# A macaron block on one core: feed-forward weights rounded in nine blocks of columns, attention masks built one level per batch, the second part's small loads first

## The chip, the core and the metric

The kernel runs on one core of a Trainium2 chip. Its time is the device time in microseconds (us) of one execution; the figure compared is the median of several executions. The core has five engines with a queue of their own: TensorE (PE), VectorE (DVE), ScalarE (ACT), GpSimd (POOL) and SyncE (SP, which here only issues DMAs). They meet through semaphores; each works through its own queue in order.

## The reference

For x of 8 batches x 512 tokens x 256 channels:

```python
x = x + 0.5 * ffn(layernorm(x))      # gate, up 256 -> 768, silu(gate) * up, down 768 -> 256
x = x + attn(layernorm(x))           # gated delta rule, 16 heads of 128
x = x + 0.5 * ffn(layernorm(x))      # the same weights again
def _quantized_matmul(x, w, scale):
    wq = w.astype(jnp.float8_e4m3fn).astype(x.dtype)
    return jnp.einsum('bsi,io->bso', x, wq) * scale
```

The attention projects to q, k, v (with a causal convolution over 4 tokens and silu), a decay alpha and a strength beta per head, runs the delta rule over the 512 tokens, normalises per head, gates and projects back. The feed-forward weights (gate, up and down, 768 KB each in float32) are rounded to 8-bit floating-point values and kept as float16.

## The kernel before, in words

`macaron` calls `ffn_phase` (first part), `attention_phase` and `ffn_phase` again (second feed-forward part; `first` is False). A barrier of all engines stands between the three. `stream` holds all of x in SBUF throughout.

**A feed-forward part** goes over 8 batches of 512 tokens. For a batch: DVE takes statistics (`stats`, L355 and L359), POOL makes 1/sqrt and shift (`root`, L271 to L276), ACT normalises (`normed`, L497), PE turns (`z_turned`, L606), ACT and DVE write it as two float16 halves (`high` L509, `low` L371). Then for each of six column blocks m of the 768: PE `gate` and `up` (L634, four 128x512 matmuls each), ACT `silu` (L517), DVE `hidden` (L380, the product with the up scale), ACT `hidden_high` (L526) and POOL `low` (L284) its two halves, PE `down` (L652). At the end DVE `added` (L391) scales and POOL `added` (L294) adds to `stream`. PE keeps three banks for gate and up; `hid`, `hh` and `hl` are rings of HB = 3. The order on each engine is written out by hand in `turn1(b)` (first part) and `turn2(b)` (second). In the first part a turn also prepares the attention for the batch before (index 1 of `root`, `normed` and so on, and the decays), and takes up to three weight jobs: SP loads a head's 128 KB into one of four slots (`load_job`, L1564), ACT splits off the high half (`high_job`, L1587 and L1589), POOL the low half (`low_job`, L1597).

**The start of the first part.** DVE rounds the three weights, one after the other, six chained instructions on 128x1536 each (L457 to L464; `s_wd` counts them), with batch 0's `low` and batch 1's statistics after the first; then the small weights of the decays (L470 to L472) and the halved down scale (L477), then `hidden(0, 0)`. SP issues the loads in the order of L156 to L187: weights, tokens, small ones, the convolution's parameters; then it waits for all the rounding (L182), saves the rounded weights to DRAM for the second feed-forward part (L183), and only then loads the first weight jobs. ACT's order in turn 0 is `silu(0,0)`, weight job 0, `silu(0,1)`, `hidden_high(0,0)`, `silu(0,2)`, `normed(0,1)`, ... POOL builds the attention's constants between `root(0,0)` and `root(0,1)`: `attention_constants`, identities, zeros and for each of six LEVELS a mask (L256 to L263).

**The start of the second feed-forward part.** SP reloads the rounded weights (L169), then the scales (L152, L172). DVE waits for the scales and halves the down scale (L476, L477) before the first statistics; ACT waits for the scales (L582) before its first `normed`.

**The attention** is a pipeline of 128 steps over all engines, one chunk of 128 tokens of four heads per step. In it the change touches the waits of PE alone: `correction` (L1415) waits for DVE's residual, `update` (L1424) for the solution and the decayed k, `check_solution` (L1403) for two semaphores, ACT's w and POOL's low half of the system.

Of the kernel before, what the change touches and what calls it, by code (L numbers as in the profile page):

```python
# [59 lines left out]
def ffn_phase(nc, first, x_in, y_out, stream, z16, kit, scratch, w):  # L60

    with ExitStack() as ctx:  # L62
# [76 lines left out]

        def rows_stored(pairs):  # L140

            return 16 * 2 * HG * pairs
# [4 lines left out]
        def _(sp):  # L147
# [7 lines left out]
            if first:  # L155
                load_x(0)  # L156
                for i, (name, rows) in enumerate((("gate_w", KT), ("up_w", KT), ("down_w", MT))):
                    sp.dma_start(wraw[:, i * KT * FF:(i + 1) * KT * FF].rearrange("p (k n) -> p k n", k=rows),
                                 w[name].rearrange("(k p) n -> p k n", p=P)).then_inc(s_w[i], 16)
                    if i == 0:  # L160
                        load_x(1)
                sp.dma_start(wab[:, :, 0:NH], w["Wa"].rearrange("(k p) n -> p k n", p=P)).then_inc(s_small, 16)
                sp.dma_start(wab[:, :, NH:], w["Wb"].rearrange("(k p) n -> p k n", p=P)).then_inc(s_small, 16)
                sp.dma_start(bab[0:NH, :], w["ba"].rearrange("(p o) -> p o", o=1)).then_inc(s_small, 16)
                sp.dma_start(bab[NH:, :], w["bb"].rearrange("(p o) -> p o", o=1)).then_inc(s_small, 16)
            else:
# [6 lines left out]
                .then_inc(s_small, 16)  # L173
            if first:
# [35 lines left out]
        def _(pool):  # L210
# [25 lines left out]
            def attention_constants():  # L236
# [15 lines left out]
                for li, mb in enumerate(LEVELS):  # L252
                    nb = P // (2 * mb)

                    blk = blocks[:, :].rearrange("p (b two m) -> p b two m", two=2, m=mb)[:, :, 0, :]
                    chain(nc.gpsimd.memset(blocks[:, :], 0.0))  # L256
                    chain(nc.gpsimd.memset(blk, -1.0))
                    fill(blk, 0.0, ALU.is_ge, -mb, [[-2 * mb, nb], [0, mb]], 1)
                    fill(blk, 0.0, ALU.is_ge, 2 * mb - 1, [[2 * mb, nb], [0, mb]], -1)
                    fill(blocks[:, :], -1.0, ALU.not_equal, 0, [[-1, P]], 1)  # L260
                    chain(nc.gpsimd.tensor_copy(kit["masks"][:, li].rearrange("p (b m) -> p b m", m=mb), blk))
                    for u in range(U):
                        chain(nc.gpsimd.tensor_copy(halves(y16[:, li, u], mb, 1), halves(kit["ident"][:, :], mb, 1)))  # L263
# [37 lines left out]
            def turn1(b):  # L301
                low(b, 0)
                root(1, b - 1)
                low(b, 1)
                weights(b, 0)
                low(b, 2)
                low(b, 3)
                weights(b, 1)
                low(b, 4)
                low(b, 5)  # L310
                root(0, b + 2)
                weights(b, 2)
                added(b)

# [10 lines left out]
            if first:  # L325
                root(0, 0)
                attention_constants()
                root(0, 1)
                for b in range(0, B + 1):
                    turn1(b)  # L330
            else:
                for b in range(-3, B + 1):
                    turn2(b)

        @block.vector
        def _(dve):
# [36 lines left out]
            def hidden(b, m):  # L373
                if not 0 <= b < B:
                    return
                q = MT * b + m
                dve.wait_ge(p_up, q + 1)
# [71 lines left out]
            if first:  # L449
                stats(0, 0)  # L450
                for i in range(3):
                    r, q = wraw[:, i * KT * FF:(i + 1) * KT * FF], wq16[:, i * KT * FF:(i + 1) * KT * FF]
                    e = wexp[:, :]
                    dve.wait_ge(s_w[i], 16)
# [10 lines left out]
                    dve.wait_ge(s_wd, i + 1)  # L465
                    if i == 0:
                        low(0, 0)
                        stats(0, 1)
# [6 lines left out]
            else:  # L475
                dve.wait_ge(s_small, 16 * 3)  # L476
            chain(nc.vector.tensor_scalar(hds[:, :], hds[:, :], 0.5, None, ALU.mult))  # L477
            if first:
                hidden(0, 0)
                hidden(0, 1)  # L480
                for b in range(0, B + 2):
                    turn1(b)
                    if b == 5:
                        attention_scales()
            else:
                for b in range(-3, B + 1):
                    turn2(b)

        @block.scalar
        def _(act):  # L490
# [20 lines left out]
            def silu(b, m):  # L511
                if not 0 <= b < B:
                    return
                q = MT * b + m
                act.wait_ge(p_gate, q + 1)
# [66 lines left out]
            act.wait_ge(s_small, 16 * (7 if first else 3))  # L582
# [6 lines left out]
        def _(pe):  # L589
# [20 lines left out]
            def gate(b, m):  # L610
                if not 0 <= b < B:
                    return
                q = MT * b + m
                if m == 0:
                    if b == 0:
                        pe.wait_ge(*((s_wd, 1) if first else (s_w[0], 16)))
                    pe.wait_ge(a_zh[0], KT * (b + 1))
                    pe.wait_ge(d_zl[0], KT * (b + 1))
# [3 lines left out]
            def up(b, m):  # L622
                if not 0 <= b < B:
                    return
                if m == 0 and b == 0:
                    pe.wait_ge(*((s_wd, 2) if first else (s_w[1], 16)))
# [12 lines left out]
            def down(b, m):  # L639
# [4 lines left out]
                pe.wait_ge(g_hl, q + 1)  # L644
                if m == 0:
                    if b == 0:
                        pe.wait_ge(*((s_wd, 4) if first else (s_w[2], 16)))
# [9 lines left out]
            def decay_products(e):  # L657

                if not 0 <= e < B:
                    return  # L660
                pe.wait_ge(a_zh[1], KT * (e + 1))
# [69 lines left out]
def attention_phase(nc, stream, z16, kit, scratch, w):  # L731

    with ExitStack() as ctx:
# [539 lines left out]
        def _(pe):  # L1273
# [5 lines left out]
            def gram_k(t):  # L1279
# [7 lines left out]
                if t > 2:  # L1287
                    pe.wait_ge(m["act_oa"], t - 2)
                else:
                    need(pe, m["dve_mix"], t)  # L1290
                    need(pe, m["act_kdec"], nk(t))
# [5 lines left out]
            def gram_q(t):  # L1297
# [7 lines left out]
                pe.wait_ge(m["dve_at"], t + 1)  # L1305
# [5 lines left out]
            def k_turned(t):  # L1311
# [3 lines left out]
                pe.wait_ge(m["dve_mix"], t + 1)  # L1315
# [65 lines left out]
            def first_solution(t):  # L1381
# [5 lines left out]
                if t > 1:  # L1387
                    pe.wait_ge(m["dve_out"], t - 1)
                else:
                    need(pe, m["dve_w"], t)  # L1390
                    need(pe, m["dve_z"], nk(t))
# [17 lines left out]
            def correction(t):  # L1409
# [3 lines left out]
                pe.wait_ge(m["dve_res"], t + 1)  # L1413
                for u in range(U):
# [3 lines left out]
            def update(t):  # L1418
# [3 lines left out]
                pe.wait_ge(m["act_kdec"], nk(t) + 1)  # L1422
                for u in range(U):
# [22 lines left out]
            def out_turned(t):  # L1446
# [3 lines left out]
                if known(t + 2) and (t + 2) % NC < NC - 1:  # L1450
                    pe.wait_ge(m["act_kdec"], nk(t + 2) + 1)
                elif known(t + 2):
                    pe.wait_ge(m["dve_mix"], t + 3)
                else:
                    pe.wait_ge(m["act_oa"], t)
# [4 lines left out]
            def output(t):  # L1460
# [7 lines left out]
                if known(t + 1) and (t + 1) % NC < NC - 1:  # L1468
                    pe.wait_ge(m["dve_z"], nk(t + 1) + 1)
                elif known(t + 1):  # L1470
                    pe.wait_ge(m["dve_w"], t + 2)
                else:
                    pe.wait_ge(m["dve_out"], t)
# [175 lines left out]
```

## Time and profile before

| | |
|---|---|
| median of 3 runs | 2579.32 us (2579.14 to 2581.09) |
| the profiled execution | 2582.29 us, its span 2580.1 us |
| PE busy in the span | 2401.2 us (93%) |
| DVE, ACT, POOL busy | 1993.1 (77%), 2018.4 (78%), 1659.0 us (64%) |
| first feed-forward part | 0 to 235.9 us |
| attention | 235.9 to 2422.4 us |
| second feed-forward part | 2422.4 to 2580.1 us |

The span is one execution as the profiler recorded it, in us from its start; what lies outside it is the difference to that execution's own time. In a timeline row the columns are start, duration, engine, line, operation, output<-inputs, shapes and how many instructions are merged; in brackets stands how long the engine was idle before it and who ended that.

### The profile page before, as it was taken

The numbers are of one execution on the slowest core, as the hardware profiler recorded it, in microseconds if no ns is written. First come the engines' busy times: TensorE is split into PE (matmuls) and PEld (weight loads), VectorE is DVE, ScalarE is ACT, GpSimd is POOL, SyncE is SP. The second block draws the span as 40 slices with busy tenths as digits, with TensorE's granted clock in tenths as the row PEclk, the third lists the DMA queues.
The fourth block names the chain that finished last, engine by engine and source line by source line (L and its number), as shares of the span: only waits on it lengthen the run. The fifth ranks groups of instructions, "written<-read, shape, count | busy, mean of one in ns | idle before, by whom it ended". The sixth has DMA issues, their size and how long they took to land. (4 is left out here: it accounts for less than half of the span.)

```text
span 2580.1 us, 64359 instructions
## 1 busy us (share of the span) xinstructions
PE 2401.2 (93%) x24496; PEld 1838.1 (71%) x24496; DVE 1993.1 (77%) x4217; ACT 2018.4 (78%) x3848; POOL 1659.0 (64%) x1929
## 2 busy tenths in 40 slices
PE   4996899999999999999999999999999999999598
PEld 2553677777777777777777777777777777777365
DVE  5555888888878788888788888888778888887254
ACT  2884788888888788888887888888888888887364
POOL 7662566666677666666676666667766666666365
PEclk8998999999999999999999999999999999999799
DMA  5000111111121011111111111111111111111001
GB/s 137 22 14 8 34 30 28 27 29 31 36 55 40 23 30 30 30 31 30 47 42 38 31 30 31 29 27 40 50 38 30 29 27 28 29 31 28 23 26 41
DMA packets 80610, 87.86 MB, mean 34 GB/s; under 512 B 21937, under 2 KB 50609, under 8 KB 80177
## 3 DMA queue, kind: packets, MB, share of 16 engines
q1 hardware_dynamic: 80304, 83.75, 12.5%
q8 instruction: 196, 3.21, 0.5%
q14 instruction: 110, 0.89, 0.1%
HBM read 77.83 MB, written 5.90 MB: 32 GB/s over the span
## 5 line engine op out<-in xcount | busy, mean ns | idle before, releaser
L1496 PE MATMUL a_bank<-k_z,k_kqv 128*128 128x512 f16 x2304 | 588.8, 380 | 11.9 <-DVE a_kb L1073 5.9
L1187 ACT ACTIVATE a_inv<-a_bank 128x512 f16<-128x512 f32 x640 | 383.8, 605 | 123.2 <-PE a_bank L1354 122.8
L1004 DVE TENSOR_TENSOR k_y<-a_bank,k_masks 128x256 f16<-128x256 f32 x768 | 320.0, 420 | 176.8 <-PE a_bank L1340 169.1
L937 POOL TENSOR_TENSOR a_oa<-a_oa,a_gb 128x512 f32<-128x512 f32 x128 | 163.2, 1275 | 303.4 <-ACT a_oa L1221 303.4
L859 POOL TENSOR_TENSOR a_am<-a_at,k_ident 128x512 f16<-128x512 f32 x128 | 162.9, 1273 | 241.1 <-DVE a_at L989 241.1
L1496 PEld LDWEIGHTS a_bank<-k_z,k_kqv 128*128 128x128 f16 x2304 | 200.9, 98 | 155.4 <-issue 17.8
L1340 PEld LDWEIGHTS a_bank<-a_inv,a_am 128*128 128x128 f16 x3072 | 164.8, 98 | 198.3 <-ACT a_inv L1187 80.9
L1073 DVE SCALAR_TENSOR_TENSOR a_kb<-a_bank,k_prm,a_kb 128x511 f32<-128x511 f32 (+2 forms) x384 | 281.0, 739 | 19.1 <-ACT a_kb L1131 15.2
L1073 DVE SCALAR_TENSOR_TENSOR a_vb<-a_bank,k_prm,a_vb 128x511 f32<-128x511 f32 (+2 forms) x384 | 280.9, 739 | 2.2 <-ACT a_vb L1131 0.6
L1073 DVE SCALAR_TENSOR_TENSOR a_qb<-a_bank,k_prm,a_qb 128x511 f32<-128x511 f32 (+2 forms) x384 | 280.6, 738 | 1.8 <-ACT a_qb L1131 1.5
L1354 PE MATMUL a_bank<-a_inv,k_y 128*128 128x64 f16 x3072 | 273.2, 193 | 0.4 <-DVE k_y L1004 0.4
L1340 PE MATMUL a_bank<-a_inv,a_am 128*128 128x64 f16 x3072 | 202.1, 194 | 53.6 <-ACT a_inv L1187 39.2
L1352 PE MATMUL a_bank<-k_y,a_inv 128*128 128x64 f16 x2560 | 237.5, 193 | 3.0 <-DVE k_y L1004 3.0
L1354 PEld LDWEIGHTS a_bank<-a_inv,k_y 128*128 128x128 f16 x3072 | 208.9, 98 | 20.3 <-DVE k_y L1004 0.5
L1352 PEld LDWEIGHTS a_bank<-k_y,a_inv 128*128 128x128 f16 x2560 | 199.6, 98 | 28.5 <-DVE k_y L1004 14.2
L1476 PE MATMUL a_bank<-k_wo,a_oh 128*128 128x256 f16 x1024 | 193.8, 277 | 20.8 <-POOL k_wo L1597 11.4
L1212 ACT ACTIVATE a_on<-a_bank,a_shift,a_rstd 128x128 f32<-128x128 f32 x512 | 193.0, 468 | 8.3 <-POOL a_shift L927 8.3
L1496 PE MATMUL a_bank<-k_z,k_gate 128*128 128x512 f16 x768 | 197.8, 382 | 0.3 <-DVE a_vb L1073 0.3
L1442 PE MATMUL a_bank<-a_wv,a_mix 128*128 128x128 f32 x1024 | 193.5, 281 | 0.2 <-DVE a_wv L1023 0.2
L905 POOL TENSOR_TENSOR a_qg<-a_qb,a_cum 128x512 f32<-128x512 f32 x96 | 113.1, 1178 | 96.1 <-PE a_bank L1442 96.1
L1441 PE MATMUL a_bank<-a_z,a_qg 128*128 128x128 f32 x768 | 164.7, 296 | 1.6 <-DVE a_wv L1023 1.6
L980 DVE TENSOR_TENSOR_SCAN a_prod<-a_decay,k_diag 128x516 f32<-128x516 f32 x128 | 157.9, 1233 | 1.1 <-ACT a_kdec L1162 1.1
(151 smaller groups left out, 6831.1 us busy)
## 6 DMA issues: line engine op xcount, KB each, us to landing
a_decay<-decay_rows SPq DMA_DIRECT2D x128, 258.0 KB, 3.3
a_cum<-cumulative_rows SPq DMA_DIRECT2D x96, 258.0 KB, 3.3
stream<-in_L_attn_x SPq DMA_DIRECT2D x8, 512.0 KB, 6.8
out<-stream SPq DMA_DIRECT2D x8, 512.0 KB, 2.9
k_raw<-in_L_attn_Wk SPq DMA_DIRECT2D x16, 128.0 KB, 3.6
k_raw<-in_L_attn_Wq SPq DMA_DIRECT2D x16, 128.0 KB, 3.4
k_raw<-in_L_attn_Wv SPq DMA_DIRECT2D x16, 128.0 KB, 2.9
k_raw<-in_L_attn_Wg SPq DMA_DIRECT2D x16, 128.0 KB, 3.5
```

The lines of the kernel that those rows point to most:

```text
L937: nc.gpsimd.tensor_tensor(oa[:, :, :], oa[:, :, :], gb[:, n % 2, :, c * C:(c + 1) * C], ALU.mult).then_inc(m["pool_og"], 1)
L1004: nc.vector.tensor_tensor(even(y16[:, j], mb), bank[LEV[par]][:, 0:U * C // 2].rearrange("p (u b m) -> p u b m", u=U, m=mb), masks[:, j].r ...
L1073: nc.vector.scalar_tensor_tensor(out=dst[:, d:S], in0=bank[PJ[j % 2]][:, 0:S - d], scalar=prm[:, i, U * (n // B) + j, TAPS - 1 - d:TAPS - ...
L1187: nc.scalar.activation(both, bank[LEV[par]][:, :].rearrange("p (two b m) -> p two b m", two=2, m=mb), ACT.Copy).then_inc(m[f"act_lev{par}" ...
L1212: ins = nc.scalar.activation(on[:, u], bank[OUT][:, u * D:(u + 1) * D], ACT.Identity, bias=shift[:, u:u + 1], scale=rstd[:, u:u + 1])
L1340: mm = pe.matmul(at_half(LEV[par], 0, u), am16[:, par, u], halves(t16[par][:, u], mb, 0), start=True, stop=True)
L1352: pe.matmul(at_half(LEV[par], 0, u), tt16[par][:, u], halves(y16[:, j, u], mb, 0), start=True, stop=True)
L1354: mm = pe.matmul(at_half(LEV[par], half, u), y16[:, j, u], halves(tt16[par][:, u], mb, 1), start=True, stop=True)
L1441: pe.matmul(units(OUT)[:, u], qg[:, u], z[:, u], start=True, stop=False)
L1442: mm = pe.matmul(units(OUT)[:, u], mix[:, t % 2, u], wv[:, u], start=not c, stop=True)
L1476: mm = pe.matmul(bank[SUM][:, 0:H], o[:, u], wo16[:, group % WO_SLOTS, wh, u], start=(u == 0 and wh == 0 and o is oh), stop=(u == U - 1 an ...
L1496: mm = pe.matmul(bank[PJ[j % 2]][:, :], wt, z16[:, zh, k, cols], start=(x == 0), stop=(x == 5))
```

## The change

Four things. The rounding is cut into nine pieces: column block pair x (0, 1, 2) of each of the three weights, 128x512 each; PE's `gate`, `up` and `down` wait for the piece that they read. The first three pieces stand ahead of `low(0,0)` and `stats(0,1)`, the other six between `hidden(0,0)` to `hidden(0,3)`. On POOL the attention's general constants move behind batch 0's `added`, and one level's constants behind each of the batches 1 to 6. On SP the first four weight jobs are issued ahead of the wait for the rounding, the saving behind them; in the second feed-forward part the scales are loaded ahead of the weights, and DVE and ACT wait for them at their first use. In the attention some waits of PE name other semaphores, or one more.

```diff
+        def third(ap, i, x):
+
+            part = ap[:, i * KT * FF:(i + 1) * KT * FF]
+            if i < 2:
+                return part.rearrange("p (k n) -> p k n", k=KT)[:, :, 2 * x * P:2 * (x + 1) * P]
+            return part.rearrange("p (m n) -> p m n", m=MT)[:, 2 * x:2 * (x + 1)]
...
         @block.sync
-            else:
-                for i in range(3):
-                    cols = slice(i * KT * FF, (i + 1) * KT * FF)
-                    sp.dma_start(wq16[:, cols], w_saved[:, cols]).then_inc(s_w[i], 16)
             load_columns(gs, "gate_scale")
             load_columns(us, "up_scale")
             sp.dma_start(hds[:, :], w["down_scale"].rearrange("(o n) -> o n", o=1).broadcast_to([P, H]))\
                 .then_inc(s_small, 16)
+            if not first:
+                for i in range(3):
+                    cols = slice(i * KT * FF, (i + 1) * KT * FF)
+                    sp.dma_start(wq16[:, cols], w_saved[:, cols]).then_inc(s_w[i], 16)
...
-                sp.wait_ge(s_wd, 4)
-                sp.dma_start(w_saved, wq16[:, :]).then_inc(s_save, 16)
                 sp.dma_start(lnwn[:, :], w["ln_w"].rearrange("(p o) -> p o", o=1)).then_inc(s_prm, 16)
                 sp.dma_start(lnb[:, :], w["ln_b"].rearrange("(p o) -> p o", o=1)).then_inc(s_prm, 16)
-                for job in range(6):
+                for job in range(4):
+                    load_job(nc, kit, w, sp, job)
+                sp.wait_ge(s_wd, 9)
+                sp.dma_start(w_saved, wq16[:, :]).then_inc(s_save, 16)
+                for job in range(4, 6):
                     load_job(nc, kit, w, sp, job)
...
         @block.gpsimd
-                for li, mb in enumerate(LEVELS):
-                    nb = P // (2 * mb)
...
+            def level_constants(li):
+
+                if not 0 <= li < NL:
+                    return
+                mb, y16 = LEVELS[li], kit["y16"]
...
             def turn1(b):
...
                 weights(b, 2)
                 added(b)
+                if b == 0:
+                    attention_constants()
+                level_constants(b - 1)
...
                 root(0, 0)
-                attention_constants()
                 root(0, 1)
...
         @block.vector
             def turn1(b):
-                hidden(b, 2)
+                if b:
+                    hidden(b, 2)
                 cumulative(b - 2)
-                hidden(b, 3)
+                if b:
+                    hidden(b, 3)
...
+                quantise(0, 0)
+                quantise(1, 0)
+                quantise(2, 0)
+                low(0, 0)
+                stats(0, 1)
+                hidden(0, 0)
+                quantise(0, 1)
+                hidden(0, 1)
+                quantise(1, 1)
+                quantise(2, 1)
+                hidden(0, 2)
+                quantise(0, 2)
+                hidden(0, 3)
+                quantise(1, 2)
+                quantise(2, 2)
...
                 for b in range(-3, B + 1):
                     turn2(b)
+                    if b == -1:
+                        dve.wait_ge(s_small, 16 * 3)
+                        chain(nc.vector.tensor_scalar(hds[:, :], hds[:, :], 0.5, None, ALU.mult))
...
         @block.scalar
-            act.wait_ge(s_small, 16 * (7 if first else 3))
...
         @block.tensor
             def gate(b, m):
+                if b == 0 and first:
+                    pe.wait_ge(s_wd, 3 * (m // 2) + 1)
...
             def correction(t):
                 pe.wait_ge(m["dve_res"], t + 1)
+                need(pe, m["act_w16"], t + 1)
...
             def update(t):
                 pe.wait_ge(m["dve_w"], t + 1)
                 pe.wait_ge(m["act_kdec"], nk(t) + 1)
+                need(pe, m["dve_w"], t + 1)
```

`quantise(i, x)` is the old chain of six instructions on `third(wraw, i, x)` and `third(wq16, i, x)`. The conditions of `up` and `down` on `s_wd` follow the same rule as those of `gate`.

**DVE at the start of the first part, before.** From the end of the rounding of the down weight (the last of 18 instructions on 128x1536) to batch 0's hidden blocks:

```order
L464 TENSOR_TENSOR f_wq<-f_wraw,f_wexp 128x1536
L470 TENSOR_SCALAR f_wab<-f_wab 128x64
L471 CAST f_wabh<-f_wab 128x64
L472 TENSOR_TENSOR f_wabl<-f_wab,f_wabh 128x64
L477 TENSOR_SCALAR f_hds<-f_hds 128x256
L380 SCALAR_TENSOR_TENSOR f_hid<-f_bank,f_us,f_sg 128x512 x6
```

**The same place in the changed kernel**, from `hidden(0, 1)` (the first row) through piece 1 of the up weight to the second of the twelve instructions up to `hidden(0, 2)`:

```order
L398 SCALAR_TENSOR_TENSOR f_hid<-f_bank,f_us,f_sg 128x512 [waits f1_act_silu,f1_pe_up,f1_weights_ready]
L480 TENSOR_SCALAR f_wexp<-f_wraw 128x512
L481 TENSOR_SCALAR f_wexp<-f_wexp 128x512 [waits f1_quantise_step]
L482 TENSOR_TENSOR f_wraw<-f_wraw,f_wexp 128x2x256 [waits f1_quantise_step]
L483 TENSOR_TENSOR f_wraw<-f_wraw,f_wexp 128x2x256 [waits f1_quantise_step]
L486 TENSOR_SCALAR f_wexp<-f_wraw 128x512 [waits f1_quantise_step]
L487 TENSOR_TENSOR f_wq<-f_wraw,f_wexp 128x2x256 [waits f1_quantise_step]
```

Five of the nine pieces, 30 instructions, now stand behind `hidden(0, 1)`, which waits for ACT's second silu; all six hidden blocks stood behind all the rounding before.

**POOL between batch 0's `added` and batch 1's first low half, in the changed kernel** (before, L294 was followed by L284 at once):

```order
L308 TENSOR_TENSOR stream<-stream,f_scaled 128x512 [waits f1_dve_y] x2
L248 MEMSET k_ident 128x128
L242 AFFINE_SELECT k_ident<-k_ident 128x128 [waits f1_pool_made]
L250 CAST k_ident<-k_ident 128x128 [waits f1_pool_made]
L251 MEMSET k_diag 128x516 [waits f1_pool_made]
L252 MEMSET k_y 128x3072 [waits f1_pool_made]
...
L242 AFFINE_SELECT k_mask0t<-k_mask0t 128x128 [waits f1_pool_made]
L298 TENSOR_TENSOR f_hl<-f_hid,f_hh 128x512 [waits f1_pe_down,f1_act_hh,f1_pool_made]
L285 TENSOR_TENSOR f_var<-f_mv,f_epsd 128x4 [waits f1_dve_mean1]
```

Twelve instructions moved into this place from the start; ten more (L256 to L263 before) now follow `added` in each of the turns 1 to 6.

## Rows read from the trace of the kernel before

**Rows 1.** Busy time of a stretch: us, PE, PEld, DVE, ACT, POOL (instructions), PE's clock, DMA share, GB/s.
```profile
40.00:50.00 10.00, 4.87 (x12) 1.64 (x12) 1.50 (x2) 2.50 (x5) 7.67 (x34) 0.60 0.24 68
```
**Rows 2.** Timeline of the first part's start, SP, ACT, DVE and PE around weight job 0.
```profile
28.93 1.72 SPq L180 DMA_DIRECT2D k_prm<-in_L_attn_vcb  x1
37.12 0.43 SPq L184 DMA_DIRECT2D k_lnwn<-in_L_attn_ln_w  x1
38.56 2.77 SPq L1564 DMA_DIRECT2D k_raw<-in_L_attn_Wk  x4
42.22 0.42 ACT L1587 ACTIVATE k_raw<-k_raw 128x256 f32<-128x256 f32 x1 [20.65 <-DMA k_raw<-in_L_attn_Wk]
43.77 0.75 DVE L380 SCALAR_TENSOR_TENSOR f_hid<-f_bank,f_us,f_sg 128x512 f32<-128x512 f32 x1 [6.07 <-ACT f_sg L517]
60.75 0.75 DVE L380 SCALAR_TENSOR_TENSOR f_hid<-f_bank,f_us,f_sg 128x512 f32<-128x512 f32 x1 [2.13 <-PE f_bank L634]
65.00 0.59 PE L634 MATMUL f_bank<-f_zh,f_wq 128*128 128x512 f16 x2
```
**Rows 3.** Timeline of DVE's rounding and of POOL beside it, and a POOL cast later, alone.
```profile
23.00 1.76 DVE L460 TENSOR_TENSOR f_wraw<-f_wraw,f_wexp 128x1536 f32<-128x1536 f32 x1
24.80 0.96 DVE L463 TENSOR_SCALAR f_wexp<-f_wraw 128x1536 f32<-128x1536 f32 x1
36.63 0.28 DVE L477 TENSOR_SCALAR f_hds<-f_hds 128x256 f32<-128x256 f32 x1
23.18 1.67 POOL L261 CAST k_masks<-f_blocks 128x64 f16<-128x64 f32 x1
38.99 0.24 POOL L261 CAST k_masks<-f_blocks 128x64 f16<-128x64 f32 x1
```
**Rows 4.** One line's instructions (ns min/median/max), and two rows late in the attention.
```profile
L980 DVE TENSOR_TENSOR_SCAN a_prod<-a_decay,k_diag x128: 1222/1224/1558, 256.6 to 2370.6; 128x516 f32<-128x516 f32 x128
2370.03 1.05 POOL L914 TENSOR_TENSOR a_zs<-a_z,a_cum 128x512 f32<-128x512 f32 x1
2370.61 1.56 DVE L980 TENSOR_TENSOR_SCAN a_prod<-a_decay,k_diag 128x516 f32<-128x516 f32 x1
```
**Rows 5.** Timeline of POOL's constants: the general ones' start and end, two levels' starts.
```profile
10.70 0.20 POOL L239 MEMSET k_ident<- 128x128 f32 x1
18.71 0.20 POOL L256 MEMSET f_blocks<- 128x128 f32 x1
43.54 0.20 POOL L256 MEMSET f_blocks<- 128x128 f32 x1
46.57 0.20 POOL L256 MEMSET f_blocks<- 128x128 f32 x1
```
**Rows 6.** Timeline of turn 1 of the first part, POOL, ACT and PE.
```profile
65.88 2.50 POOL L294 TENSOR_TENSOR stream<-stream,f_scaled 128x512 f32<-128x512 f32 x2
69.07 1.16 POOL L284 TENSOR_TENSOR f_hl<-f_hid,f_hh 128x512 f16<-128x512 f32 x1 [0.68 <-ACT f_hh L526]
71.21 0.20 POOL L271 TENSOR_TENSOR f_var<-f_mv,f_epsd 128x4 f32<-128x4 f32 x1 [0.98 <-DVE f_mv L359]
71.90 0.27 PE L652 MATMUL f_bank<-f_wq,f_hh 128*128 128x256 f16 x1
72.74 0.20 POOL L276 TENSOR_TENSOR f_shift<-f_nmean,f_rstd 128x4 f32<-128x4 f32 x1
74.44 2.06 ACT L497 ACTIVATE f_ztok<-stream,f_shift,f_rstd 128x256 f32<-128x256 f32 x4
76.55 1.09 PE L606 MATMUL f_bank<-f_ident,f_ztok 128*128 128x128 f32 x8 [1.02 <-ACT f_ztok L497]
```
**Rows 7.** Timeline of the second feed-forward part's start, SP and DVE.
```profile
2424.83 1.01 SPq L172 DMA_DIRECT2D f_hds<-in_L_ffn_down_scale  x1
2429.24 1.41 DVE L355 BATCH_NORM_STATS2 f_bn<-stream 128x6 f32<-128x256 f32 x4
```
**Rows 8.** Timeline of the attention's end: PE behind two semaphores.
```profile
2402.13 0.23 PE L1403 MATMUL a_bank<-a_rhs,a_am 128*128 128x128 f16 x1 [0.93 <-ACT a_rhs L1204]
```

More of the change, by code:

```diff
@@ L251, in attention_constants @@
                 fill(mask0t[:, :], -1.0, ALU.not_equal, 0, [[-1, P]], 1)
-                for li, mb in enumerate(LEVELS):
-                    nb = P // (2 * mb)
[L255 to L263, printed above, removed]
+            def level_constants(li):
+                if not 0 <= li < NL:
+                    return
+                mb, y16 = LEVELS[li], kit["y16"]
+                nb = P // (2 * mb)
+                blk = blocks[:, :].rearrange("p (b two m) -> p b two m", two=2, m=mb)[:, :, 0, :]
+                chain(nc.gpsimd.memset(blocks[:, :], 0.0))
+                chain(nc.gpsimd.memset(blk, -1.0))
+                fill(blk, 0.0, ALU.is_ge, -mb, [[-2 * mb, nb], [0, mb]], 1)
+                fill(blk, 0.0, ALU.is_ge, 2 * mb - 1, [[2 * mb, nb], [0, mb]], -1)
+                fill(blocks[:, :], -1.0, ALU.not_equal, 0, [[-1, P]], 1)
+                chain(nc.gpsimd.tensor_copy(kit["masks"][:, li].rearrange("p (b m) -> p b m", m=mb), blk))
+                for u in range(U):
+                    chain(nc.gpsimd.tensor_copy(halves(y16[:, li, u], mb, 1), halves(kit["ident"][:, :], mb, 1)))
             def root(n, e):
@@ L376, in hidden @@
                 q = MT * b + m
+                if q == 0:
+                    dve.wait_ge(s_small, 16 * (7 if first else 3))
                 dve.wait_ge(p_up, q + 1)
@@ L450, in _, with quantise @@
                 stats(0, 0)
[L451 to L454, printed above, removed]
+                def quantise(i, x):
+                    r, q = third(wraw, i, x), third(wq16, i, x)
+                    e = wexp[:, 0:KT * 2 * P].rearrange("p (k n) -> p k n", k=KT)
+                    if x == 0:
+                        dve.wait_ge(s_w[i], 16)
                     chain(nc.vector.tensor_scalar(e.bitcast(I32), r.bitcast(I32), 0x7F800000, None, ALU.bitwise_and))
@@ L514, in silu @@
                 q = MT * b + m
+                if q == 0:
+                    act.wait_ge(s_small, 16 * (7 if first else 3))
                 act.wait_ge(p_gate, q + 1)
@@ L624, in up @@
                     return
-                if m == 0 and b == 0:
-                    pe.wait_ge(*((s_wd, 2) if first else (s_w[1], 16)))
+                if b == 0 and first:
+                    pe.wait_ge(s_wd, 3 * (m // 2) + 2)
+                elif b == 0 and m == 0:
+                    pe.wait_ge(s_w[1], 16)
                 need(pe, a_sg, MT * b + m)
@@ L644, in down @@
                 pe.wait_ge(g_hl, q + 1)
+                if b == 0 and first:
+                    pe.wait_ge(s_wd, 3 * (m // 2) + 3)
+                elif b == 0 and m == 0:
+                    pe.wait_ge(s_w[2], 16)
                 if m == 0:
-                    if b == 0:
-                        pe.wait_ge(*((s_wd, 4) if first else (s_w[2], 16)))
                     need(pe, d_y, KT * b)
@@ L1314, in k_turned @@
                 n, c = divmod(t, NC)
-                pe.wait_ge(m["dve_mix"], t + 1)
+                need(pe, m["dve_mix"], t + 1)
                 for u in range(U):
```

57 lines of the change are left out of this document (31 added, 26 removed).

## The prediction

> **What bounds the kernel.** The page comes first: PE is busy for 93% of the span, so there is something to win only where PE waits. The busy time by stretch shows such a place at the start: from 40 to 50 us PE has 4.87 us of work, and its clock is granted at 0.60 on average [rows 1]. The timeline there shows the chain. SP issues the first weight job's load at 38.56, behind the wait for all the rounding; ACT stands before that job for 20.65 us, until 42.22; its second silu is behind it in its queue, so `hidden(0,1)` starts at 43.77. `normed(0,1)` then waits for POOL's root, which stands behind all the constants. The sixth hidden block starts at 60.75, and PE begins batch 1 at 65.00 [rows 2]. From there the turns repeat. The second feed-forward part, which begins at 2422.4, opens with a wait of DVE: its first statistics start at 2429.24, behind the down scale [rows 7].
>
> **The second feed-forward part: -6.7, +0.1.** `stats(0,0)` no longer waits for a load. It starts with the barrier, at 2422.5 for 2429.24: 6.7 us earlier [rows 7]. Statistics, root, `normed`, turning and the halves follow as a chain of some 10 us before PE's first gate, so that comes at about 2433. The reloads of the weights now stand behind three small ones, the last of them an issue of 1.01 [rows 7], so some 2 us later; they were never waited for, and are in time even if they take 8 us. ACT's table load for silu now stands behind the wait for PE's first gate: about 1.3 us later for one silu, nearly all covered, since DVE waits at that place for PE's `up` anyway; I take 0.1. Bounds: -6.8 to -5.5.
>
> **The start of the first part: +2.1.** In SP's new order `ln_w` follows the last parameter load (28.93 + 1.72 = 30.65), and the jobs' loads follow `ln_w` by 38.56 - 37.12 = 1.44: 32.1. ACT began the job 42.22 - 38.56 = 3.66 after the issue, so now at 35.8, 6.4 earlier [rows 2]. `hidden(0,1)` moves to 37.3 and ends at 38.05. But five of the nine pieces stand behind it in DVE's queue; before, all the rounding lay inside ACT's wait. A piece has three single-input instructions of 512 columns, 0.42 each (between 0.28 for 256 and 0.96 for 1536), three with two inputs, 0.69 each (1.76 for 1536, a third of it and a fixed part of 0.16), and six gaps of 0.03 to 0.04 (the rows at 23.00 and 24.80): 3.5 us [rows 3]. Five are 17.5, two hidden blocks 1.5 [rows 2], four small instructions of 0.28 at most, with gaps, 1.0 [rows 3]. `hidden(0,4)` could start at 38.05 + 17.5 + 1.5 + 1.0 = 58.1.
>
> *POOL holds DVE there.* In that stretch POOL has four low halves of 1.16 [rows 6] and two weight jobs, half as wide, some 0.67, to do. Beside the rounding a POOL cast of 0.24 was stretched to 1.67 while DVE's instruction of 1.76 ran; it ended at 24.85, just after that one, and the next of DVE, from 24.80, kept its 0.96 [rows 3]. So POOL gets in between two instructions, and 0.24 fits without a loss. The other way round, the scan that starts at 2370.61 under a POOL instruction which runs until 2371.08 takes 1.56 for 1.22: DVE loses what is left of POOL's, less 0.14 [rows 4]. I take 0.33 of each POOL instruction as free (0.24, and 0.14 less the 0.05 by which the cast reached over), the rest as DVE's loss: 4 x 0.83 + 2 x 0.34 = 4.0. `hidden(0,4)` then starts at 62.1, `hidden(0,5)` 0.8 later; from there to batch 1 on PE it was 65.00 - 60.75 = 4.25 [rows 2], so that begins at 67.1, **2.1 later**. Bounds: with no loss DVE would allow 63.1, and PE, on its lower clock after its waits [rows 1], would need until 63.2 to 64.6, 1.2 earlier on the middle; with a loss of their whole length, 6.0, it is 4.1 later. I am nearer to the scan's row than to the cast's, for these POOL instructions are as long as the scan's neighbour.
>
> The Trainium skill, "SBUF — State Buffer", section "Who interferes with whom", speaks against this part of the change: a VectorE instruction with two SBUF inputs or in a two-port mode and a GpSimd instruction that reads SBUF exclude each other, and whichever starts first holds the other up for its whole length. By that rule alone the start would be at the upper bound, +4.1; the scan's row agrees with it on who waits and takes a little off.
>
> **The constants on POOL: +3.0, +1.0.** At the start they delayed root; that is in the numbers above. The general ones took 18.71 - 10.70 = 8.0 [rows 5], of which I take 1.9 for two short instructions stretched by DVE as the cast was: 6.1 where they stand now. In turn 1 POOL was free of `added(0)` at 65.88 + 2.50 - 65.00 = 3.4 after PE began the batch; now at 9.5. A low half of 1.16 and root (71.21 to 72.94, 1.73) follow, so `normed(1,0)` can start at 12.4 to 12.5. It started 74.44 - 65.00 = 9.44 after, and PE already waited for it (1.02) [rows 6]: 3.0 late, and PE with it. DVE's fourth hidden block, which needs the low half, is late by less. Bounds: 2.5 and 4.9.
>
> A level takes 46.57 - 43.54 = 3.03 [rows 5]. In each of the turns 2 to 7 POOL has 0.6 to 0.7 idle before the low half, and 0.98 before root [rows 6] (turn 1 shows the pattern of all). So the low half is 2.4 late and ends 7.7 after the batch's start, 0.8 after PE stood at `down` (71.90 - 65.00 = 6.9), which PE has as idle 1.02 just behind; root is 1.5 late, and `normed` had 74.44 - 72.94 = 1.5 in hand [rows 6]. All just covered: 0.1 per turn and 0.5 for the first level's short pieces, 1.0. Bounds: 0 and 2.4 each.
>
> **The attention: 0.** `correction` gets a second semaphore, long up, 128 times; `check_solution` has two, and its wait ends with ACT's output alone [rows 8]. Bounds: 0 and 0.03 each, +3.8.
>
> **Sum.** 2.1 + 3.0 + 1.0 - 6.7 + 0.1 = -0.5. The profiled execution (2582.29, 3.0 above the median of the runs shown, and above their highest) would come to 2581.8; on the median of 2579.3 it is **2578.8 us**. 0.2% of this kernel, 5.2 us, is about what a measurement can tell from no change; so this is no change, since the first part gives back what the second wins.
>
> **Rivals.** *DVE is not held* (0.27): POOL slips between the pieces as the cast did, and batch 1 starts 1.2 earlier: 2579.3 - 1.2 + 3.0 + 1.0 - 6.6 = 2575.5. For it: no instruction of the rounding shown was longer beside POOL [rows 3]. Against: the scan [rows 4].
> *The levels close a loop over POOL* (0.11), the one that ends slower. Its place is POOL between `added(b)` and the next low half in the turns 2 to 7. If root, `normed` and `z_turned` have less in hand than I read, a level costs 1 to 2.4 and not 0.15: 2578.8 + 6 x 0.85 = 2583.9 to 2578.8 + 6 x 2.25 = 2592.3; I name 2586. It decides from 1.0 per level. Against it stands PE's idle 1.02; for it, that every cover is used up to the last tenth.
> *The second wait costs* (0.05): 0.03 each gives 2582.6.
> *The new start works as written* (0.09): job 0's load lands some 3 us before 35.8, because SP's issues ahead of it shrink, and DVE is not held: 2575.5 - 3 = 2572.5. Against: nothing in front of those issues has changed.
>
> **How the numbers follow.** The forecast has 0.48, with 2575.5 to 2582.5 as its own range. The whole range reaches to the fourth rival, 2572.5, and over the lower end of the second, to 2584.5. Faster by over 0.2% (under 2574.2): most of the fourth, a third of the first and the edge of the forecast, 0.24. Slower (over 2584.5): most of the second and a little of the rest, 0.11. Within: 0.65.
>
> **What would show it.** The second part's first statistics at its barrier, and its length 151 for 157.7 us. ACT's job 0 at 35.8, `hidden(0,1)` at 37.3; `hidden(0,4)` at 62 if DVE is held, at 58 if not, with instructions of the pieces that took 1.2 or 1.5 for 0.42 or 0.69; batch 1 on PE at 67.1. Turn 1 longer by 3, PE standing 3 to 4 us before its first `down`; the turns 2 to 7 within 0.2 of their old length. If batch 1 begins before 64 or the later turns grow by 1, the prediction is wrong in its middle.

## Result and profile after

| | before | after |
|---|---|---|
| median of 6 runs each | 2581.2 us | 2589.59 us |
| lowest to highest | 2579.14 to 2581.91 | 2586.97 to 2594.04 |
| profiled execution (span) | 2582.29 (2580.1) | 2594.04 (2592.3) |
| PE, DVE busy | 2401.2, 1993.1 | 2405.1, 2005.4 |
| first part, to the attention's first matmul | 235.93 | 254.99 |
| attention, to its last addition on `stream` | 2186.0 | 2186.3 |
| the rest | 158.2 | 151.0 |

The ratio is 1.0037, interval 1.0024 to 1.0050: the change makes the kernel slower by 0.37%. The forecast was no change, -0.5 us in the sum of its terms; the medians lie 8.4 apart. The profiled execution of after is the longest of its six, 4.5 above their median; this matters below. The last three rows of the table add up to its span: +19.1, +0.3 and -7.2 make the +12.2 between the spans.

The second part did what it was meant to. Its first statistics, which answer to those of [rows 7], follow the attention's last addition at once, and its gain is there in full (DVE of after):

```profile
2440.88 0.42 DVE L1104 SCALAR_TENSOR_TENSOR stream<-a_bank,stream 128x256 f32<-128x256 f32 x1 [7.28 <-PE a_bank L1532]
2441.86 1.41 DVE L371 BATCH_NORM_STATS2 f_bn<-stream 128x6 f32<-128x256 f32 x4 [0.55 <-PEq L777]
...
2453.76 0.26 DVE L522 TENSOR_SCALAR f_hds<-f_hds 128x256 f32<-128x256 f32 x1
```

So 19.1 us are lost in the first part. The start, on SP, ACT and DVE of after, answers to [rows 2]:

```profile
33.42 1.97 SPq L1620 DMA_DIRECT2D k_raw<-in_L_attn_Wk  x4
...
35.72 0.42 ACT L1643 ACTIVATE k_raw<-k_raw 128x256 f32<-128x256 f32 x1 [12.86 <-DMA k_raw<-in_L_attn_Wk]
...
37.30 0.75 DVE L398 SCALAR_TENSOR_TENSOR f_hid<-f_bank,f_us,f_sg 128x512 f32<-128x512 f32 x1 [10.11 <-ACT f_sg L554]
37.96 1.23 DVE L480 TENSOR_SCALAR f_wexp<-f_wraw 128x512 int32<-128x512 int32 x1
39.23 0.43 DVE L481 TENSOR_SCALAR f_wexp<-f_wexp 128x512 f32<-128x512 f32 x1
...
48.65 1.61 DVE L482 TENSOR_TENSOR f_wraw<-f_wraw,f_wexp 128x512 f32<-128x512 f32 x1
...
62.10 0.75 DVE L398 SCALAR_TENSOR_TENSOR f_hid<-f_bank,f_us,f_sg 128x512 f32<-128x512 f32 x1
64.06 0.75 DVE L398 SCALAR_TENSOR_TENSOR f_hid<-f_bank,f_us,f_sg 128x512 f32<-128x512 f32 x1 [1.21 <-PE f_bank L674]
```

The row at 37.96 is an instruction of 0.43 that took 1.23, beside POOL's first low half at 37.76; the one at 48.65 took 1.61 for 0.69. There are six of these, with 0.80, 0.83, 0.35, 0.92, 0.83 and 0.35 too much: 4.1 us. Each is what was left of POOL's instruction when DVE's began, less 0.14 to 0.16. The hidden block at 64.06 waits for PE, which worked from 57.64 to 63 on its lower clock (two matmuls 1.06 for 0.59), and PE begins batch 1 at 68.31 where it was 65.00.

In turn 1, POOL's general constants stand where they were put, and this is what PE and ACT wait for:

```profile
71.63 0.22 POOL L248 MEMSET k_ident<- 128x128 f32 x1
...
77.74 1.15 POOL L298 TENSOR_TENSOR f_hl<-f_hid,f_hh 128x512 f16<-128x512 f32 x1
...
78.95 0.28 PE L694 MATMUL f_bank<-f_wq,f_hh 128*128 128x256 f16 x1 [3.58 <-POOL f_hl L298]
...
80.64 1.58 ACT L532 ACTIVATE f_ztok<-stream,f_shift,f_rstd 128x256 f32<-128x256 f32 x3 [2.80 <-POOL f_shift L290]
```

The length of a turn is read between two starts of `added` on POOL:

| turn | 1 | 2 | 3 | 4 | 5 | 6 | 7 |
|---|---|---|---|---|---|---|---|
| before | 20.90 | 21.20 | 21.21 | 21.19 | 21.21 | 22.88 | 19.09 |
| after | 24.55 | 22.38 | 22.36 | 23.79 | 23.77 | 23.74 | 22.87 |

Turn 1 costs 3.65: PE stands idle for 3.58 us in it instead of 1.56, and its busy time is 20.97 instead of 19.34, at a granted clock of 0.93 instead of 1.00. The turns 2 to 7, with one level each, cost 12.1 together. Turn 4 shows why, first before:

```profile
132.29 1.16 POOL L284 TENSOR_TENSOR f_hl<-f_hid,f_hh 128x512 f16<-128x512 f32 x1 [0.60 <-ACT f_hh L526]
...
134.43 0.20 POOL L271 TENSOR_TENSOR f_var<-f_mv,f_epsd 128x4 f32<-128x4 f32 x1 [0.98 <-DVE f_mv L359]
...
134.85 1.02 POOL L274 TENSOR_TENSOR f_rstd<-f_var,f_nhalf 128x4 f32<-128x4 f32 x1
...
134.90 1.23 DVE L403 TENSOR_TENSOR_SCAN f_gx<-f_ab,f_heads 16x516 f32<-16x516 f32 x1
```

and the same place in after:

```profile
142.86 1.14 POOL L277 CAST k_y<-k_ident 128x64 f16<-128x64 f32 x4
...
144.09 1.15 POOL L298 TENSOR_TENSOR f_hl<-f_hid,f_hh 128x512 f16<-128x512 f32 x1
...
144.19 2.13 DVE L421 TENSOR_TENSOR_SCAN f_gx<-f_ab,f_heads 16x516 f32<-16x516 f32 x1
...
145.20 1.12 POOL L285 TENSOR_TENSOR f_var<-f_mv,f_epsd 128x4 f32<-128x4 f32 x1
...
145.30 0.28 PE L694 MATMUL f_bank<-f_wq,f_hh 128*128 128x256 f16 x1 [0.72 <-POOL f_hl L298]
...
147.89 2.07 ACT L532 ACTIVATE f_ztok<-stream,f_shift,f_rstd 128x256 f32<-128x256 f32 x4 [0.84 <-POOL f_shift L290]
...
150.01 1.09 PE L642 MATMUL f_bank<-f_ident,f_ztok 128*128 128x128 f32 x8 [1.08 <-ACT f_ztok L532]
```

Before, the low half had been done for about 1.4 us when DVE came to its cumulative scan. Now the late low half meets it. The low half holds the scan (2.13 for 1.23), and the scan then holds root's first instruction until 146.32 (1.12 for 0.20). Root begins 1.5 late, as foretold, and ends 2.4 late; only 1.5 were in hand, so `normed` starts 9.41 after `added` where it started 8.47 after it. In the turns 2 and 3 the scan came first and the low half was held (at 99.69, 1.95 for 1.16, PE waiting 1.86). This much costs 1.2 a turn (turns 2 and 3). The rest is PE's clock, by stretch in after (columns: span of the stretch, busy time of PE, its weight loads, DVE, ACT and POOL, granted clock, DMA share, GB/s):

```profile
116.00:138.50 22.50, 20.50 (x128) 12.49 (x127) 12.86 (x32) 18.52 (x33) 17.79 (x30) 1.00 0.08 22
138.50:162.30 23.80, 22.00 (x128) 12.98 (x126) 13.63 (x31) 18.64 (x33) 17.58 (x30) 0.93 0.08 20
162.30:186.00 23.70, 21.96 (x128) 13.00 (x126) 13.49 (x31) 18.63 (x33) 17.47 (x29) 0.93 0.06 15
```

In each of the turns 4 to 7 a part runs at the clock's lower level, and PE is busy 1.6 to 1.7 longer for the same work. Of the turns before, that happened in turn 6 alone.

Turn 7 is a case of its own. In the kernel before, ACT stands there for root, and PE has no wait at `z_turned`; the 1.5 and the 1.02 that the other turns have in hand are missing:

```profile
201.46 2.08 ACT L497 ACTIVATE f_ztok<-stream,f_shift,f_rstd 128x256 f32<-128x256 f32 x4 [0.52 <-POOL f_shift L276]
...
203.87 1.04 PE L606 MATMUL f_bank<-f_ident,f_ztok 128*128 128x128 f32 x8
```

### The profile page after: what moved, and what is told of

It is laid out like the page before. It is cut to its first block and busy times, and to the rows that moved or that the text cites. A ratio compares the mean times of both kernels' runs of the same rounds, so it can differ in the third digit from the quotient of the medians.

```text
span 2592.3 us, 64538 instructions
## 1 busy us (share of the span) xinstructions
PE 2405.1 (93%) x24496; PEld 1836.4 (71%) x24496; DVE 2005.4 (77%) x4253; ACT 2019.6 (78%) x3848; POOL 1651.4 (64%) x1929
## 5 line engine op out<-in xcount | busy, mean ns | idle before, releaser
L1117 DVE SCALAR_TENSOR_TENSOR a_kb<-a_bank,k_prm,a_kb 128x511 f32<-128x511 f32 (+2 forms) x384 | 280.9, 738 | 19.1 <-ACT a_kb L1175 15.2
L298 POOL TENSOR_TENSOR f_hl<-f_hid,f_hh 128x512 f16<-128x512 f32 x96 | 112.8, 1181 | 89.6 <-ACT f_hh L563 89.0
```

The lines of the kernel that those rows point to most:

```text
L1117: nc.vector.scalar_tensor_tensor(out=dst[:, d:S], in0=bank[PJ[j % 2]][:, 0:S - d], scalar=prm[:, i, U * (n // B) + j, TAPS - 1 - d:TAPS - ...
```

## Experiments

The theory after these traces: the second part wins 7; the new start costs 2 to 3, the general constants 3.7; the levels cost the rest, and they do so by their place ahead of DVE's scan. Turn lengths below are from one profiled execution each. The ratios are to the kernel before; its medians beside the runs were 2578.76 us (runs 1 to 4), 2578.32 (5 to 8) and 2579.61 (9 to 11). Differences to the kernel before are worked out from the ratios.

**1. The second part alone.** The kernel before, with these lines of the change:

```diff
+                if q == 0 and not first:
+                    dve.wait_ge(s_small, 16 * 3)
...
-            else:
-                dve.wait_ge(s_small, 16 * 3)
-            chain(nc.vector.tensor_scalar(hds[:, :], hds[:, :], 0.5, None, ALU.mult))
...
+                    if b == -1:
+                        dve.wait_ge(s_small, 16 * 3)
+                        chain(nc.vector.tensor_scalar(hds[:, :], hds[:, :], 0.5, None, ALU.mult))
...
+                if q == 0 and not first:
+                    act.wait_ge(s_small, 16 * 3)
```

(and the loads of the weights on SP behind the small ones).

> The kernel before with the change of the second feed-forward part alone. The theory (the second part wins 6.7 to 7.1 us, and all the loss lies in the first) expects 2581.2 - 7 = 2574.2 us, a ratio of 0.9973 to the kernel before. The rival that part of the loss lies in the second part or in what it does to the attention expects under 4 us, 2577 or more.

Measured: 2571.74 us, ratio 0.9972 (0.9964 to 0.9981), -7.2 us; the stretch behind the attention is 150.9. The second part wins in full, so the loss lies ahead of it.

**2. The general constants back.**

```diff
-                if b == 0:
-                    attention_constants()
                 level_constants(b - 1)
...
                 root(0, 0)
+                attention_constants()
                 root(0, 1)
```

> The changed kernel with the general constants back on POOL ahead of root(0,1); the six levels stay in the turns 2 to 7. Theory (turn 1 costs 3.65 by itself, the levels about 12, independent of each other): 2589.6 - 3.7 = 2585.9 us, turn 1 back to 20.9 us, turns 2 to 7 longer than before by 1.2 or 2.6 each as now. Rival (the levels are harmless, and the later turns are slow as a consequence of turn 1's delay): turns 2 to 7 return to 21.2 and the time falls by 12 to 15, to 2575 to 2578.

Measured: 2583.59 us, ratio 1.0025 (1.0014 to 1.0036). Turn 1 is 20.78; the turns 2 to 7 stay long: 22.37, 22.36, 22.14, 22.10, 22.05, 21.19. The rival falls. Here the clock is at 1.00 in all these turns:

```profile
109.70:132.00 22.30, 20.30 (x128) 12.34 (x126) 12.65 (x31) 18.53 (x33) 17.76 (x29) 1.00 0.08 22
132.00:154.20 22.20, 20.41 (x128) 12.41 (x127) 13.56 (x31) 18.52 (x33) 17.58 (x30) 1.00 0.08 22
154.20:176.30 22.10, 20.36 (x128) 12.38 (x126) 13.47 (x31) 18.53 (x33) 17.51 (x30) 1.00 0.06 16
```

So this execution gives the levels' cost by itself: the six turns are 132.2, and before they are 126.8 with 1.7 of a lower clock in turn 6, so 125.1: 7.1 us for six levels: 0.9 to 1.2 in each of the turns 2 to 6, and 2.1 in turn 7. The 12.1 of after's profile hold up to 5 more of the clock, which differs from one execution to the next; the runs of this kernel spread from 2579.73 to 2591.6, and the profiled one is the fastest of the twelve.

**3. All constants at the start.**

```diff
-                if b == 0:
-                    attention_constants()
-                level_constants(b - 1)
...
                 root(0, 0)
+                attention_constants()
+                level_constants(0)
+                level_constants(1)
                 root(0, 1)
+                for li in range(2, NL):
+                    level_constants(li)
```

> The changed kernel with general constants and all six levels at POOL's start: general ones and levels 0 and 1 between root(0,0) and root(0,1), levels 2 to 5 behind it, in POOL's idle stretch before the first low half. Theory: turns 1 to 7 as in the kernel before (20.9, 21.2 ...), so 2589.6 - 3.7 - 12 = 2574 us; the first low half slips by about 2 us, which costs nothing, since DVE is the later there. Rival (the start of the changed kernel and the clock are what cost, not the levels): 2585 or more.

Measured: 2577.45 us, ratio 0.9997 (0.9988 to 1.0006). The turns are as before (20.90, 21.20, 22.88, 21.20, 21.20, 21.21, 19.08), so it is the constants' place in the turns that costs, but the time is 3 us above what I expected. I had taken the levels at 12 from a profile that lay 4.5 above its kernel's median. With 7.1 the expectation is 2589.6 - 3.65 - 7.1 = 2578.9, a ratio of 0.9991, which the interval holds.

**4. The attention's waits alone.** The kernel before with the changed attention, for instance:

```diff
                 pe.wait_ge(m["dve_res"], t + 1)
+                need(pe, m["act_w16"], t + 1)
```

> The kernel before with the changed waits of the attention alone. The theory (the waits cost nothing; in the trace the attention's stretch is 0.2 us longer) expects a ratio of 1.000, 2581.2 us. The rival of the prediction, a second wait of 0.03 us each, expects +3.8, 2585.

Measured: 2580.98 us, ratio 1.0008 (1.0000 to 1.0017). Inconclusive by itself; run 10 takes it up.

**5 and 6. A short scan, after and before.** The scan of both kernels cut to 4 columns; `gx` is filled with 1.0 once, so the decay products are left out.

```diff
-                nc.vector.tensor_tensor_scan(gx[:, g].rearrange("p c x -> p (c x)"),
...
+                nc.vector.tensor_tensor_scan(gx[:, g, 0, 0:4], ab[0:NH, g, 0, 0:4], heads0[:, 0, 0:4],
+                                             0.0, ALU.mult, ALU.add).then_inc(d_g, 1)
```

> The changed kernel with the cumulative scan of DVE cut from 516 columns to 4; the rest of its result is a constant, so the decay products are left out. Levels stay in the turns 2 to 7. Theory (a level's own 2.5 us are covered but for a tenth or two, as the prediction said, and what breaks the cover is the scan, whose 1.2 us now fall on POOL's late low half or on its root): low half back to 1.16 from 1.95 or 2.13, root's first instruction back to 0.20 from 1.12, turns 2 to 6 at 21.3 to 21.5 us instead of 22.4, so 5 to 6 us less than the changed kernel, a ratio to the kernel before of 1.0010 to 1.0020. Rival (the level's length alone breaks it): turns stay at 22.1 or more, and the ratio at 1.003 or more.

> The kernel before with the same short scan, to see whether the scan costs anything where no level stands in the turns; the decay products are left out here too. Both theories: turns at 21.2 us as before, a ratio of 1.000. Were it 0.998 or less, the scan would cost by itself, and the run before this one would say nothing of the levels.

Measured, after with the short scan: 2578.26 us, ratio 0.9999 (0.9990 to 1.0008), some 10 us below the changed kernel, and faster than the 1.0010 to 1.0020 that were expected. Before with it: 2578.28 us, 1.0000 (0.9991 to 1.0009). The scan costs nothing by itself. Without it the levels cost 1.7 us instead of 7.1: turns 2 to 6 are 21.58, 21.37, 21.22, 21.21 and 21.20, next to nothing; turn 7 is 20.26, still 1.2 above before's. The 10 us are more than these 5.4; the clock, at 1.00 in all six turns here, is a part of them. Turn 3 of the run with levels and short scan:

```profile
117.60 1.14 POOL L277 CAST k_y<-k_ident 128x64 f16<-128x64 f32 x4
...
118.83 1.16 POOL L298 TENSOR_TENSOR f_hl<-f_hid,f_hh 128x512 f16<-128x512 f32 x1
...
119.94 0.20 POOL L285 TENSOR_TENSOR f_var<-f_mv,f_epsd 128x4 f32<-128x4 f32 x1
...
120.04 0.28 PE L693 MATMUL f_bank<-f_wq,f_hh 128*128 128x256 f16 x1 [0.85 <-POOL f_hl L298]
...
123.84 1.09 PE L641 MATMUL f_bank<-f_ident,f_ztok 128*128 128x128 f32 x8 [0.17 <-ACT f_ztok L531]
```

This is the picture that the prediction had drawn: PE waits 0.85 at the first `down` and gets it back at `z_turned`, where 0.17 is left of 1.02. It is right for the turns 2 to 6 of a kernel without the scan.

**11. The level elsewhere in the turn.**

```diff
                 low(b, 3)
                 weights(b, 1)
+                level_constants(b - 2)
                 low(b, 4)
...
-                level_constants(b - 1)
```

> The changed kernel with the level of a turn moved behind low(b, 3), where POOL waits 1.8 us for the next low half and DVE has no scan; general constants stay in turn 1. Theory (place, not length, makes a level dear): turns 2 to 7 at 21.2 to 21.5 us, 6 to 10 us less than the changed kernel, a ratio to the kernel before of 1.000 to 1.0015. Rival (2.5 us more on POOL cost 1.2 wherever they stand in the turn): 1.003 or more.

Measured: 2581.3 us, ratio 1.0003 (0.9994 to 1.0012). Turns 2 to 7: 21.44, 22.64, 21.20, 21.20, 22.82, 19.09; the two long ones have the clock at 0.92. The same work on the same engine is free half a turn later, because nothing of POOL's then meets the scan:

```profile
118.53 1.02 POOL L288 TENSOR_TENSOR f_rstd<-f_var,f_nhalf 128x4 f32<-128x4 f32 x1
118.57 1.23 DVE L421 TENSOR_TENSOR_SCAN f_gx<-f_ab,f_heads 16x516 f32<-16x516 f32 x1
...
128.34 1.14 POOL L277 CAST k_y<-k_ident 128x64 f16<-128x64 f32 x4
129.56 2.32 POOL L298 TENSOR_TENSOR f_hl<-f_hid,f_hh 128x512 f16<-128x512 f32 x2
```

**7. The first weight jobs' loads early.** Run 3, and:

```diff
             if first:
+                for job in range(4):
+                    load_job(nc, kit, w, sp, job)
                 for b in range(2, B):
                     load_x(b)
...
-                for job in range(4):
-                    load_job(nc, kit, w, sp, job)
```

> The changed kernel with all constants at POOL's start (as in the run of that name) and the first four weight jobs' loads issued right behind the last small load, ahead of the token loads. Theory (DVE stands 10 us in the start because ACT waits for job 0's load): job 0 runs at about 23, hidden(0,1) starts at 27 instead of 37, but POOL's constants, which end at about 39, now hold the first low half and with it PE's first down product; 7 us of the 10 are won: 2577.5 - 7 = 2570.5 us, ratio 0.997. Rival (DVE's rounding is held up by POOL's constants, since both now run through the whole start): no gain, 0.9995.

Measured: 2571.8 us, ratio 0.9969 (0.9959 to 0.9978). DVE's idle time before `hidden(0,1)`, 7.90 in run 3 and 10.11 in after, is gone (`hidden(0,1)` at 28.63), and `added(0)` starts at 62.42 for 67.55. PE now waits for POOL, as expected, and DVE then stands for 3.76 behind the same low half:

```profile
44.29 0.40 PE L696 MATMUL f_bank<-f_wq,f_hh 128*128 128x256 f16 x1 [7.18 <-POOL f_hl L298]
```

**8. Levels between the low halves.**

```diff
                 low(b, 0)
+                if b == 0:
+                    level_constants(1)
...
                 low(b, 3)
+                if b == 0:
+                    level_constants(4)
+                    level_constants(5)
```

(with levels 2 and 3 ahead of and behind `low(b, 2)`, and level 0 at the start).

> The changed kernel with the four loads early, general constants and level 0 at POOL's start, and the other five levels between the low halves of turn 0, where POOL waits for DVE's rounding. Theory: the first low half isn't held, batch 1 starts on PE at about 57 instead of 68, turns 1 to 7 are as in the kernel before: 10 us less than with all constants at the start, 2567 us, ratio 0.9955. Rival (levels beside rounding hold DVE): batch 1 at 60 or later, ratio 0.997 or more.

Measured: 2570.16 us, ratio 0.9971 (0.9961 to 0.9982): a miss, no better than run 7. DVE is done with the rounding at 51.8, three earlier than in run 7, but levels 4 and 5 hold the fifth low half. The rival's two figures came (0.9971, and batch 1 on PE after 62), but not its cause: beside the levels DVE lost some 0.2.

```profile
56.07 1.14 POOL L277 CAST k_y<-k_ident 128x64 f16<-128x64 f32 x4
57.30 0.67 POOL L1661 TENSOR_TENSOR k_kqv<-k_raw,k_kqv 128x256 f16<-128x256 f32 x1
57.92 2.27 POOL L298 TENSOR_TENSOR f_hl<-f_hid,f_hh 128x512 f16<-128x512 f32 x2
```

**9. The last level in turn 1,** where there is no scan yet. Run 8, and:

```diff
                     level_constants(4)
-                    level_constants(5)
...
                 added(b)
+                if b == 0:
+                    level_constants(5)
```

> As the run with the levels between the low halves, but the last level behind added(0), in turn 1, where DVE has no scan yet. Theory: the fifth low half of batch 0 starts at about 54.5 instead of 57.9 and batch 1 on PE 3 us earlier; the one level in turn 1 costs 0.1 to 0.4, since no scan stands there: 2567 us, a ratio to the kernel before of 0.996. Rival (a level costs 1.2 or more in any turn): ratio 0.9965 or more and turn 1 at 22 us or more.

Measured: 2567.68 us, ratio 0.9948 (0.9935 to 0.9962). The low half starts at 54.94, `added(0)` at 59.47 for 63.13, and turn 1 with its level is 20.74, for 20.90 in the kernel before: the level is free there.

```profile
54.94 2.27 POOL L298 TENSOR_TENSOR f_hl<-f_hid,f_hh 128x512 f16<-128x512 f32 x2
...
59.47 2.50 POOL L308 TENSOR_TENSOR stream<-stream,f_scaled 128x512 f32<-128x512 f32 x2
```

This version beats both kernels: 13 us less than before, some 23 less than the changed one.

**10. Run 9 with the attention of before.** The lines of run 4 are undone.

> The run above with the attention's waits as in the kernel before. Theory (the waits cost nothing; PE's idle time in the attention is 77 to 79 us in every run, with them and without): the same time, a ratio between the two of 1.000. Rival (they cost about 2 us, as the run with them alone might say, 1.0008): 2 us less than the run above.

Measured: 2569.57 us, ratio 0.9958 (0.9946 to 0.9971). Without the changed waits it is not faster; by these medians it is 1.9 slower, where run 4 had the changed waits 2 slower. Times of this spread can't settle 2 us either way. The profiles say more. The attention's length differs by itself: 2183.1 to 2189.4 over thirteen profiles, with the old waits 2183.1, 2183.4, 2186.0 and 2186.6. PE's idle time in it is 97.2 to 98.5 with the old waits (four profiles) and 95.8 to 99.5 with the changed ones (nine), 97.7 on average in both. So the changed waits cost PE nothing that can be seen; what differs is its busy time for the same 22656 matmuls, 2085.8 to 2090.4.

## Why the prediction was wrong

- **"The second feed-forward part: -6.7, +0.1"** was right: -7.2 in the profile and -7.2 alone (run 1), 0.4 more than the bound of -6.8. The first statistics come 0.56 after the attention's last addition, for 7.3; 0.3 of the rest is PE's busy time in the part, 135.04 for 135.38, at a clock of 0.94 for 0.92.
- **"The start of the first part: +2.1"** was right in its mechanism and 1.2 small in after's profile. Job 0 at 35.72 (35.8), `hidden(0,1)` at 37.30 (37.3), `hidden(0,4)` at 62.10 (62.1), DVE's loss 4.1 (4.0). So the rival that DVE is not held is out. That the first two agree to a tenth is luck: the load was issued at 33.42 and not at 32.1, and ACT began 2.30 after the issue and not 3.66. In four other profiles with this start job 0 begins at 34.15 to 34.89. What was missing: PE's `gate`, `up` and first `down` products behind its wait ran on the lower clock until 63, so `hidden(0,5)` waited 1.21 for PE. Five profiles with this start have `added(0)` at 66.54 to 69.19 with 67.13 in the middle, and four with before's start have it at 64.68 to 65.88 with 65.6 in the middle: 1.5 apart, so 2.1 is a fair size and after's 3.3 the largest seen.
- **"The constants on POOL: +3.0"** for turn 1 was right in kind: 3.65, and 6.1 for the constants as foretold; run 2 takes it away. `normed` started 12.33 after the batch (12.4 foretold), but PE did not wait for it: behind its 3.58 at `down` PE ran on the lower clock and came to `z_turned` later than `normed` let it. Of the 3.65, 2.0 are idle time and 1.6 busy time of PE. The same turn is 24.52 at 0.93 in the profiles of runs 5 and 11, and 20.74 to 21.22 at 1.00 in all ten profiles without the wait of 3.58.
- **"The constants on POOL: +1.0"** for the six levels is the step that failed. It measured 7.1 with the clock undisturbed and 12.1 in after's profile. It lies in the range of the second rival, "the levels close a loop over POOL": 1.2 a level of its 1 to 2.4, near the 1.35 that its named 2586 comes to, and I had given it 0.11. It had place and size, but not the cause. The sum of durations was right: root did start 1.5 late, and the low half 2.5 (2.4 foretold). The error lay in "root is 1.5 late, and `normed` had 1.5 in hand": a cover used to the last tenth was checked against POOL's own queue only. I had counted how POOL holds DVE at the start, and had read the scan's row for it [rows 4], but did not lay the moved instructions over DVE's scan in these turns, where the hold goes both ways and returns 0.9 to POOL. The scan accounts for 5.4 of the 7.1 (run 5). A second error is "turn 1 shows the pattern of all": turn 7 has neither the 1.5 nor the 1.02 in hand, and 1.2 of the remaining 1.7 fall there.
- **PE's clock** stood in no term of the turns. In after's profile it fell in four of the six turns with a level, and a turn became about 1.6 longer again; in run 2's, with the same waits, it fell in none. It also falls in one or two turns of the kernels whose turns have no new waits, so that the waits bring it on is likely in turn 1 and not shown in the others. Nor is a wider spread of after shown: its six runs lie within 7 us for 2.8 of the kernel before, but 35 runs of the kernel before lie within 9.6.
- **"The attention: 0"** holds by PE's idle time (runs 4 and 10); the times alone leave some 2 us open, and no run shows the 0.03 a wait of the rival.

Put together by after's own profile: 3.3 + 3.65 + 12.1 + 0.3 - 7.2 = 12.2, its difference in span. On the medians the difference is 8.4. The sum does not close everywhere: from the start's 1.5 to 2.1 and the second part's -7.2, run 3 should have a ratio of 0.998, and it has 0.9997 (0.9988 to 1.0006). In its profile the attention is 4.5 longer than in run 1's, 4.4 of that as PE's busy time, which points to PE's clock. Why it should be lower there is open.

## What to carry to other kernels

Work moved onto an engine "with idle time" has to be laid over what the engine that it can hold up does at that minute, not only over its own queue: here 2.5 us cost nothing at the start (run 3), in turn 1 (run 9) and in the middle of a turn (run 11), and 0.9 to 2.1 behind `added`, more with PE's clock. A pattern read in one turn has to be looked for in the last one too. A cover that comes out at exactly zero is no cover; price the next collision, and PE's clock behind it. And when a profile is used to size a term, compare its own time with the median first.

## Not expected of the hardware

The hold between DVE and POOL goes by the kind of instruction, also where POOL only writes. In run 7, beside one POOL memset of 2.82, DVE's two-input instructions kept their 0.69 and its single-input one took 1.39 for 0.43:

```profile
11.31 2.82 POOL L252 MEMSET k_y<- 128x3072 f16 x1
11.57 0.69 DVE L484 TENSOR_TENSOR f_wraw<-f_wraw,f_wexp 128x512 f32<-128x512 f32 x1
12.29 0.69 DVE L485 TENSOR_TENSOR f_wraw<-f_wraw,f_wexp 128x512 f32<-128x512 f32 x1
13.02 1.39 DVE L488 TENSOR_SCALAR f_wexp<-f_wraw 128x512 f32<-128x512 f32 x1
```

It ended at 14.41, just behind the memset. The Trainium skill, "SBUF — State Buffer", section "Who interferes with whom", says this: two SBUF inputs contend with a GpSimd instruction that reads SBUF and not with one that only writes, a two-port mode with either. By that the trace agrees, for both kinds, if the single-input instruction runs in a two-port mode, which the trace does not tell. What does not fit the rule is seen in turn 4 of before, shown above: POOL's `rstd` (134.85, 1.02) and DVE's scan (134.90, 1.23) ran side by side and neither was stretched, while root's first instruction of after was held from 145.20 to the scan's end. Why the one is let through and the other not is open.
